# A graph network's segment sums on one core: degree matmuls moved beside the 64-wide feature matmuls, one matmul dropped, edge loads let go from the start

## What is computed

```
h   = relu(layernorm(x))
agg = segment_sum(edge_attr_64 @ W_edge.T, dst) / clip(degree(dst), 1)
x   = x + concat([h @ W_self.T, agg @ W_neigh.T]) @ W_final.T + b_final
h   = relu(layernorm(x))
agg = segment_sum(edge_attr_128, dst)
x   = x + relu(concat([h, agg]) @ W1 + b1) @ W2 + b2
```

## Time and profile before

| | us |
|---|---|
| median of three runs | 629.72 |
| lowest and highest run | 625.45, 639.87 |
| profiled execution, span of the program | 629.2 |
| from the start to PE's first edge matmul | 19.7 |
| edge phase, to PE's last edge matmul, about | 487 |
| last phase and end, about | 122 |

### The profile page before, as it was taken

How to read it: one execution, slowest core, us unless ns; L and a number is a source line. 1 busy time by engine, 2 the same in 40 slices (tenths; PEclk the granted TensorE clock), 3 DMA queues, 4 the chain that set the end, 5 groups by cost and what they waited for, 6 DMA issues and landing times.

```text
span 629.2 us, 32293 instructions
## 1 busy us (share of the span) xinstructions
PE 573.6 (91%) x11415; PEld 512.2 (81%) x11415; DVE 397.7 (63%) x1474; ACT 297.6 (47%) x617; POOL 150.5 (24%) x161
## 2 busy tenths in 40 slices
PE   6998999989999899999899999999999857999996
PEld 5988889889888889889889888888988845777774
DVE  7755556656656556665665665566665537888883
ACT  1344454454554454554554544454531004777774
POOL 9312122122122022122122112122111003444441
PEclk9999999999999999999999999999999967999999
DMA  5999999999999999999999999999999900222222
GB/s 148 310 323 336 333 306 344 329 322 315 338 316 338 327 323 320 345 321 325 309 324 349 319 327 336 340 328 326 324 316 342 304 16 4 66 66 66 66 68 74
DMA packets 169882, 168.17 MB, mean 267 GB/s; under 512 B 9979, under 2 KB 169858, under 8 KB 169858
## 3 DMA queue, kind: packets, MB, share of 16 engines
q1 hardware_dynamic: 155120, 160.84, 79.3%
q10 hardware_dynamic: 14738, 7.03, 3.8%
HBM read 161.42 MB, written 6.40 MB: 267 GB/s over the span
## 4 chain that ended last, share of the span: by engine, by line
DMA 41%; PE 22%; issue 16%; ACT 9%; DVE 7%; DVEq 4%; ACTq 1%; SPq 1%
DMA xn<-in_x_dram 37%; ACT hn L573 4%; PE ps L521 4%; PE ps L500 4%; PE ps L506 4%; PE ps L508 4%; DMA ring<-in_edge_attr_dram 3%; DVEq L732 2%; ACT std L568 2%; PE ps L434 2%; DVE mv L724 2%; PE ps L440 2%; PE ps L514 2%; ACT minus_mean L567 2%; DVE bn L718 1%
## 5 line engine op out<-in xcount | busy, mean ns | idle before, releaser
L434 PE MATMUL ps<-onehot,ring 128*64 128x64 f32 x3126 | 231.6, 224 | 27.4 <-DVE onehot L701 22.5
L434 PEld LDWEIGHTS ps<-onehot,ring 128*64 128x64 f32 x3126 | 202.1, 137 | 48.1 <-DVE agg L710 31.7
L436 PE MATMUL ps<-onehot,ring 128*64 128x64 f32 x3126 | 234.6, 225 | 0.4 <-issue 0.4
L440 PE MATMUL ps<-onehot,ring 128*64 128x64 f32 x3126 | 225.3, 222 | 1.8 <-issue 1.8
L710 DVE TENSOR_TENSOR agg<-ps,agg 128x128 f32 x521 | 150.0, 288 | 106.8 <-DVE agg L710 72.7
L440 PEld LDWEIGHTS ps<-onehot,ring 128*64 128x64 f32 x3126 | 203.3, 138 | 2.0 <-issue 2.0
L436 PEld LDWEIGHTS ps<-onehot,ring 128*64 128x64 f32 x3126 | 201.9, 137 | 0.1
L701 DVE TENSOR_TENSOR onehot<-iota_win,rel 128x384 f32<-128x384 f32 x261 | 143.8, 552 | 0.0
L352 POOL TENSOR_TENSOR x<-x,xb 128x256 f32 (+1 forms) x49 | 49.7, 1015 | 329.6 <-ACT x L588 329.6
L447 PE MATMUL ps<-onehot,ones_h 128*64 128x128 bf16 (+1 forms) x783 | 87.5, 219 | 0.0
L443 PE MATMUL ps<-onehot,ones_h 128*64 128x256 bf16 x261 | 77.5, 297 | 0.0
(11 more groups left out here) (87 smaller groups left out, 576.5 us busy)
## 6 DMA issues: line engine op xcount, KB each, us to landing
ring<-in_edge_attr_dram SPq DMA_DIRECT2D x260, 384.0 KB, 4.5
ring<-in_edge_attr_dram SPq DMA_DIRECT2D x260, 192.0 KB, 5.1
xn<-in_x_dram ACTq DMA_DIRECT2D x48, 128.0 KB
out_dram<-ring SPq DMA_DIRECT2D x24, 256.0 KB, 2.3
x<-in_dst_dram SPq DMA_DIRECT2D x1, 768.0 KB
ring<-in_edge_attr_dram SPq DMA_DIRECT2D x1, 159.0 KB
x<-in_L_gnn_W_final_dram ACTq DMA_DIRECT2D x1, 128.0 KB, 4.6
ring<-in_edge_attr_dram SPq DMA_DIRECT2D x1, 79.5 KB
```

The costliest lines, as they stand in the source:

```text
L434: nc.tensor.matmul(totals[0:H, b, 0, :], ring128[:, slot, b, r * D:r * D + H], hots[:, b, r, :], start=first, stop=final)
L436: nc.tensor.matmul(totals[H:P, b, 0, :], ring128[:, slot, b, r * D + H:(r + 1) * D], hots[:, b, r, :], start=first, stop=final)
L440: nc.tensor.matmul(totals[H:P, b, 1, :], ring64[:, slot, b, r * D64:(r + 1) * D64], hots[:, b, r, :], start=r == 0, stop=r == RUN - 1)
```

## The change

The credit of five chunks is given by PE's first instruction, ahead of its wait for the constants, so SP issues the first five chunks' loads right behind those of `dst`. The matmul whose result nobody reads is gone. The degree matmuls are six instead of three, each over one batch (64 columns instead of 128), and each stands right behind the L440 matmul of the same batch and run, in the other column half. The last degree matmul still raises `s_mm`.

```diff
-        KEEPERS = 1
...
+            pe.sem_inc(s_mm, C_MM)
             pe.wait_ge(s_const, N_CONST)
             warm_up()
             turn_tables(1)
...
             last.then_inc(s_turn, 1)
-            pe.sem_inc(s_mm, C_MM)
...
                 for b in range(batches):
                     for r in range(RUN):
+                        first, final = r == 0, r == RUN - 1
                         nc.tensor.matmul(totals[H:P, b, 1, :], ring64[:, slot, b, r * D64:(r + 1) * D64], hots[:, b, r, :],
-                                         start=r == 0, stop=r == RUN - 1)
-                for i in range(KEEPERS):
-                    nc.tensor.matmul(ps_w[0:H, 0:256], ones_h[:], onehot[:, slot, :, :].bitcast(BF16).rearrange("p t n -> p (t n)")[:, 0:256],
-                                     start=True, stop=True)
-                for r in range(RUN):
-
-                    last = nc.tensor.matmul(totals[0:H, 0:batches, 1, :], ones_h[:], halves[:, 0:batches, r, :, 1],
-                                            start=r == 0, stop=r == RUN - 1)
+                                         start=first, stop=final)
+                        last = nc.tensor.matmul(totals[0:H, b, 1, :], ones_h[:], halves[:, b, r, :, 1],
+                                                start=first, stop=final)
                 last.then_inc(s_mm, 1)
```

## The result

Over 21 runs each, the changed kernel takes 631.8 us (628.82 to 644.04) and the kernel before 628.79 (625.45 to 641.09): ratio 1.004, 95% interval 1.0021 to 1.006, so about 2.5 us slower. That lies within 2% and within the range, but the sum of the prediction had 0.9 us less than before (628.3 against 629.2), and the direction is wrong. Where its head is concerned I read a second copy of the same kernel beside it (run `again`, span 628.2).

What follows compares the result with a forecast made beforehand. It took each edge-phase turn to be bound by about 4.1 us plus the landing of x. The terms 629.2 - 1.1 - 0.1 + 0.3 gave 628.3, predicted as 628 us, range 616 to 640.

Steps and rivals of the forecast that it cites:

- The bound: Edge phase: a turn is about 4.1 us plus the landing of x, 9.43 us on average.
- The degree matmuls: PE's edge chunks: L440 keeps 58 ns, a turn's PE floor falls 0.26 us to 8.26; -1.1 us in all.
- rival A: Edge chunks, L440's slots: interleaved bf16 matmuls take a slot each, 0.35 us per chunk; +41 us, 670; chance 0.07.
- The credit: Head: earlier edge loads gain 0 and may delay weights; +0.3 us, ends 0 and +4.2.
- The sum: Whole kernel: 629.2 - 1.1 - 0.1 + 0.3 = 628.3 us; the 0.1 is the last chunk's tail.
- B, the clock: Edge phase: without the unread matmul the clock is low, phase over 300 us longer; chance 0.03.
- C, the balance: Edge-phase turns: smoother PE chunks let transfers reach 355 GB/s, 592 us, or fill PE's gaps, 616; chance 0.13.
- D: Head: weights land late for PE, up to 4.2 us, 632; no separate chance, inside the forecast's 0.77.

Runs made afterwards that it cites:

- experiments 1 to 3: First: the changed kernel again and its parts apart. Second: code shifted by instructions that never run. Third: POOL's clearing of agg against DVE in the head.
- credit: The kernel before with the early credit alone: 629.3 us, ratio 0.9979.
- before_shift236: The kernel before with 236 instructions more in PE's branch that never runs: 632.01 us, ratio 1.0056.
- before_port: The kernel before, with POOL's second clearing of agg waiting until DVE has made rel_f: 626.94 us, ratio 0.9992.
- before_one_memset: The kernel before, with POOL clearing its part of agg by one memset instead of two: 638.85 us, ratio 1.0169.
- pe_only: The changed kernel with the credit back at its old place: 641.16 us, ratio 1.0075.
- after_shift24: The changed kernel with 24 instructions more in PE's branch that never runs: 629.04 us, ratio 0.997.
- after_shift24_port: The changed kernel with 24 instructions more that never run and POOL's second memset waiting for DVE's rel_f: 627.6 us, ratio 1.0007 to the kernel before.
- nokeep_port: before_port without the unread matmul, with 124 instructions more that never run: 625.16 us, ratio 0.9969 to the kernel before.
- nokeep_credit: nokeep_port with the early credit added: 624.45 us, ratio 0.9946 to the kernel before.
- experiments 1 to 4: experiments 1 to 3 plus a fourth that took dropping the unread matmul and interleaving the degree matmuls apart.
- x_early: before_port with the load of x issued ahead of ACT's square root and DVE's second statistics moved from chunk 2 to 3: 601.19 us, ratio 0.9583 to the kernel before.
- inter_port: after_shift24_port with the credit back at its old place: 627.12 us, ratio 0.9981 to the kernel before.

## Why the prediction was right or wrong

*The bound* was right. The turn went by the landing of `x` plus a fixed piece; taking 1.3 us of table load and the statistics out of that piece took 0.6 us and more off every turn (8.73 for 9.34 to 9.43). The window's 355 GB/s, from which I had a turn of 8.7 us as the next floor, came out as 353 GB/s and 8.73. In after the turn stayed at 9.34 us, within the 9.3 to 9.5 that I had given, but DVE's wait for `x` didn't stay near 60 us (41.9). A small misreading: the pieces for `x` in the chain of before take 4.12 to 6.83 us, not 4.3 to 6.6.

*The degree matmuls* were right in mechanism; their size isn't shown. L440 keeps its 58 ns, a direct chunk takes 1.40 us, L442 runs beside it; rival A falls. I had put 1.1 us for it. From PE's first matmul of chunk 25 to that of chunk 245, by the timelines, the five kernels of experiments 1 to 3 with the old PE part (before, `credit`, `before_shift236`, `before_port`, `before_one_memset`) took 413.99, 411.45, 412.08, 412.65 and 413.04 us, mean 412.6; those with the new one (after, `again`, `pe_only`, `after_shift24`, `after_shift24_port`) 411.21, 409.98, 412.92, 410.47 and 413.20, mean 411.6. The means differ by 1.1 us, and the single ones spread by more than that, so the match is partly luck. The two highest of the new ones are the two with 3.4 us at half the clock in this stretch. And dropping the unread matmul alone gives more: 407.27 in `nokeep_port`, 407.58 in `nokeep_credit`. I had valued it only by its 0.13 us of the lower half and hadn't asked what the interleaving takes back. In whole times the gain of 0.9 us that the sum has doesn't show either: with position and race taken out after is at 627.6 and before at 626.94.

*The credit* was right: no gain, and 0 to 0.7 us in the head from one execution to the next. The weights landed later, `b_col` after 7.9 instead of 3.1 us, at about 13 us: between the 8.2 of an even share and the 17.2 of all in order of issue. The rule of turns between queues of the Trainium skill, which I had weighed ("DMA: Bandwidth & Descriptors", Queues, rings and completion order), gave 0; the trace doesn't agree that the small weights slip past the edges, but for the time that was hardly worse than my 0.3.

*The sum* failed. "629.2 - 1.1 - 0.1 + 0.3 = 628.3": the sum has a term for everything that PE executes and none for the program itself. I counted the two more matmuls of a chunk as free since they run beside others, and never asked what it does that 60 texts of a chunk grow by four instructions each. The missing term is +3.2 us at the change to the last phase (5.75 to 8.94). With it the change is -1.1 - 0.1 + 0.3 + 3.2 = +2.3 us, against the 2.5 measured (1.3 to 3.8 by the interval); as the -1.1 is not shown, that it comes out so close is luck. In the turns that run once PE's waits for "issue" are longer, too, 3.4 to 5.3 us in the six interleaved kernels of experiments 1 to 4 against 1.8 to 4.5 in the five with the old PE part, but no longer time from chunk 245 to the last edge matmul goes with it (28.1 to 30.4 us against 27.9 to 30.9). The sign of it stood in the trace of before: PE waited 2.2 us for "issue" in the edge phase, and DVE stood 4.02 us like this at the very change of phase.

*The rivals.* A didn't occur. B, the clock, didn't in after in the stretch that I had named, with 1.00 from 60 to 460 us; short half-clock stretches do occur in single executions of kernels without the unread matmul. C, the balance, didn't come with this change. That the transfers can run at 353 GB/s is shown by `x_early`, at 601 us, but it got there by a shorter fixed piece and not by PE's chunks. D was 0.19 us of its 4.2 in `again` and 0.7 in `after_shift24_port`.

## What to carry to other kernels

Count what a change adds to an engine's program as well as what it adds to its time: where the program goes from a loop into text that runs once, look for waits that "issue" ends, and before believing a difference of half a per cent, shift the code by some instructions that never run. Where a profile says that a turn is a transfer's landing plus a fixed piece, shorten that piece, not the engine that waits behind it: here that was worth 26 us, and all that was done to PE's matmuls 2.5 us or less either way. And where runs of one kernel spread by 3%, compare the heads of two executions from its two ends before calling it chance.

## What the hardware showed that I had not expected

- PE's wait at the change of phase is 5.8 or 8.8 us according to where its code lies, and 24 instructions decided it here. More code was loaded by the queue for instructions in after than before (15 packets, 0.25 MB, against 13 and 0.21), but `after_shift24` and `before_shift236` both have 14 and 0.23 MB, so that count doesn't tell which.
- Beside a memset by POOL, which reads nothing, two DVE operations ended 10.7 us late, L660 (one input) and L661 (two). The page on SBUF of the Trainium skill ("SBUF — State Buffer", SBUF: two separate sides) has a DVE operation with two inputs contend only with a GpSimd operation that reads SBUF, and one in a two-port mode with any; the rows show one that only writes, and no run shows in which mode the two work, nor which of them was held.
- The same pair of engines meets in most turns, at POOL's addition (L351, L352 before) and a one-hot table of DVE. First before, where DVE is first and POOL takes 1.07 instead of 0.73 us, then after, where POOL is 0.02 us ahead and DVE takes 1.12 instead of 0.55:

```profile
107.19 0.55 DVE L701 TENSOR_TENSOR onehot<-iota_win,rel 128x384 f32<-128x384 f32 x1
107.26 1.07 POOL L352 TENSOR_TENSOR x<-x,xb 128x256 f32 x1 [6.64 <-ACT x L588]
```

```profile
108.09 0.73 POOL L351 TENSOR_TENSOR x<-x,xb 128x256 f32 x1 [6.57 <-ACT x L583]
108.11 1.12 DVE L696 TENSOR_TENSOR onehot<-iota_win,rel 128x384 f32<-128x384 f32 x1
```

In none of the 49 turns with this addition does it go the second way in the five kernels of experiments 1 to 3 with the old PE part, but in 26 of them in after, in 28 in `again`, and in 10 to 23 in the other six of experiments 1 to 4 without the unread matmul. Nearly all of after's 15.3 us more of one-hot tables is this (26 x 0.57 = 14.8). What it costs in time no run shows: `inter_port` and `nokeep_credit` have 14 each and differ by 2.5 us in the turns.

- The second warm-up takes 3.81 or 5.44 us from one execution to the next: with a granted clock of 1.00 throughout, or of 0.53 for 3.6 us of it (`again`, from 16.4 us).
- 353 GB/s was what one core's edge phase reached with nothing else in the way, in four kernels with different PE programs.
